# A transpose one place later in the job list, and a stage change without store waits, in an attention and FFN block

## The reference, cut to what matters

```python
xn = layernorm(x)                                  # x: 8 x 1024 x 512
# attention heads (head width 128)
local  = softmax(q_l k_l^T * s) v_l                # qkv = xn @ local_qkv_w
sparse = softmax(top102(q_s k_s^T * s)) v_s        # keeps the 102 largest scores of each row
xp     = xn @ memory_proj_w
w      = softmax(xp @ memory_bank^T)               # 64 memory slots: "memory weights"
mem    = concat(xp, w @ memory_bank) @ mem_out_w + mem_out_b
pred   = gelu((xn @ pred_in_w + b) @ pred1_w + b) @ pred2_w + b
s = concat(local, sparse, mem, pred) @ warboss_w + warboss_b
# FFN over the same xn, hidden width 2048
g = silu(relu(xn @ w1 + b1) @ w2 + b2)
out = x + s * g
```

## Time and profile before

| | |
|---|---|
| time, median of 3 runs | 2635.92 us (2635.5 to 2636.25) |
| the profiled execution's own time | 2635.15 us |
| its span, first to last instruction | 2633.3 us |
| TensorE busy | 2550.7 us, 97% |
| VectorE busy | 2308.2 us, 88% |
| ScalarE busy | 1367.4 us, 52% |
| GpSimd busy | 1102.4 us, 42% |
| mean granted TensorE clock | 0.993 |
| mean DMA rate | 214 GB/s |

### The profile page before, as it was taken

How to read it: one execution, slowest core, us unless ns; L and a number is a source line. 1 busy time by engine, 2 the same in 40 slices (tenths; PEclk the granted TensorE clock), 3 DMA queues, 4 the chain that set the end, 5 groups by cost and what they waited for, 6 DMA issues and landing times.

```text
span 2633.3 us, 37059 instructions
## 1 busy us (share of the span) xinstructions
PE 2550.7 (97%) x12900; PEld 2145.8 (81%) x12900; DVE 2308.2 (88%) x5217; ACT 1367.4 (52%) x2311; POOL 1102.4 (42%) x863
## 2 busy tenths in 40 slices
PE   6999999969999999999999999999999999999998
PEld 5887788757888888888888888888888888888886
DVE  7555555569999999999999999999999999999996
ACT  5777777734444444444444444444444444445443
POOL 4444444423344444444444444444444444444444
PEclk9999999989999999999999999999999999999999
DMA  6777777794556455655564556456655655465554
GB/s 214 289 288 291 291 271 272 275 355 148 192 183 238 167 194 192 226 173 195 202 230 166 192 196 229 160 199 212 211 179 183 235 189 197 164 241 175 195 168 165
DMA packets 168555, 562.29 MB, mean 214 GB/s; under 512 B 18161, under 2 KB 31665, under 8 KB 159921
## 3 DMA queue, kind: packets, MB, share of 16 engines
q1 hardware_dynamic: 168368, 559.91, 60.6%
HBM read 425.63 MB, written 134.22 MB: 213 GB/s over the span
## 4 chain that ended last, share of the span: by engine, by line
PE 76%; DVE 2%; DMA 1%; POOL 0%; issue 0%; ACT 0%; POOLq 0%; SPq 0%
PE acc L60 9%; PE acc L58 9%; PE hid L58 9%; PE hid L60 9%; PE acc L59 9%; PE hid L59 9%; PE o L60 5%; PE o L58 4%; PE o L59 4%; PE scores L1248 4%; PE scores L60 2%; PE scores L59 2%; PE scores L58 2%; DVE larger L1164 1%; DVE top_l L1144 1%; DMA w1s<-ffn_scratch 0%
## 5 line engine op out<-in xcount | busy, mean ns | idle before, releaser
L1004 POOL TENSOR_TENSOR h_lo<-h,h_hi 128x512 fp32r<-128x512 f32 x256 | 332.8, 1300 | 884.5 <-ACT h_hi L902 884.5
L1144 DVE MAX8 top_l<-larger 128x8 f32<-128x512 f32 x832 | 573.8, 690 | 13.2
L1164 DVE MATCH_REPLACE8 larger<-top_l,larger 128x512 f32<-128x512 f32 x768 | 519.3, 676 | 0.0
L901 ACT ACTIVATE h<-hid,b 128x512 f32<-128x512 f32 x256 | 176.7, 690 | 489.6 <-PE hid L60 489.6
L58 PE MATMUL acc<-w2s,h_hi 128*128 128x512 f32 x1024 | 412.1, 402 | 0.0
L58 PE MATMUL hid<-xnT,w1s 128*128 128x512 f32 x1024 | 400.4, 391 | 5.3 <-DMA w1s<-ffn_scratch 3.2
L60 PE MATMUL acc<-w2s,h_lo 128*128 128x512 f32 x1024 | 401.6, 392 | 0.0
L59 PE MATMUL acc<-w2s,h_hi 128*128 128x512 f32 x1024 | 400.2, 391 | 0.0
L60 PE MATMUL hid<-xnT,w1s 128*128 128x512 f32 x1024 | 400.1, 391 | 0.0
L59 PE MATMUL hid<-xnT,w1s 128*128 128x512 f32 x1024 | 399.2, 390 | 0.0
L1004 POOL TENSOR_TENSOR pT_s<-pT,pT_s 128x512 fp32r<-128x512 f32 x256 | 326.4, 1297 | 51.8 <-ACT pT_s L914 51.8
(11 more groups left out here) (170 smaller groups left out, 5575.4 us busy)
## 6 DMA issues: line engine op xcount, KB each, us to landing
w2s<-ffn_scratch SPq DMA_DIRECT2D x259, 512.0 KB, 3.9
w1s<-ffn_scratch SPq DMA_DIRECT2D x258, 512.0 KB, 4.5
kv<-kv_scratch SPq DMA_DIRECT2D x34, 1024.0 KB, 6.6
xnT<-xnT_scratch SPq DMA_DIRECT2D x68, 512.0 KB, 8.0
tl<-tile_scratch SPq DMA_DIRECT2D x66, 512.0 KB, 3.9
xnT_scratch<-xnT SPq DMA_DIRECT2D x16, 2048.0 KB, 13.6
kv_scratch<-kv_out SPq DMA_DIRECT2D x32, 1024.0 KB, 6.3
tile_scratch<-tiles_out SPq DMA_DIRECT2D x16, 2048.0 KB, 7.7
```

Of the source, the lines that this page charges most:

```text
L901: nc.scalar.activation(h32[:, c % 2, :], hid[:, :], ACT.Relu, bias=bias)
L1004: return nc.gpsimd.tensor_tensor(out_, value, hi_.bitcast(F32), ALU.subtract).then_inc(ready, 1)
L1144: l_step = count(nc.vector.max(top_l[:, own], larger[:, :]))
L1164: l_step = count(nc.vector.match_replace(larger[:, :], top_l[:, own], larger[:, :], LOWEST))
```

## The change

- `wt` stands behind `kl` in `JOBS`, not ahead of it. The other engines' written orders stay as they are.
- Stage 1 no longer waits for its stores to land. The semaphores of the K/V and tile stores live in both stages, and stage 2 waits on them ahead of the loads that read the last stores.
- In the last half (n = `LAST` = 15): no input load and no layer norm; behind the FFN store, and ahead of the tile store, SyncE loads stage 2's tile 0, K sparse of batch 0 and W1 chunk 0 into buffers that both stages share (`load_first`); there is no further FFN load; VectorE, not GpSimd, subtracts for `v23`.
- xnT is one buffer of both stages; half 0, which the last transposes leave there, isn't loaded again.
- Stage 2's first loads go in the order W1 chunk 1, (wait for the tile stores), W2 chunk 0, K local, W2 chunk 1, tile 1, (wait for the K/V stores). The other W2 chunk follows in the loop, and the loads of xnT move from tiles 0 and 4 of a batch to tiles 1 and 5.

```diff
-JOBS = ["mp", "pi", "ql", "ms", "p1a", "p1b", "qs", "wt", "kl", "ks", "p2",
+JOBS = ["mp", "pi", "ql", "ms", "p1a", "p1b", "qs", "kl", "wt", "ks", "p2",
...
+                def load_first():
+
+                    sp.wait_ge(kv_st, 32 * LAST)
+                    sp.wait_ge(tiles_st, 16 * LAST)
+                    loads = ((shared.tl0[:, :, :, :].rearrange("p i s n -> p (i s n)"),
+                              tile_d[0, :, :, :, :].rearrange("p i s n -> p (i s n)")),
+                             (shared.ks[:, :, :, :].rearrange("p u s n -> p (u s n)"),
+                              kv_d[0, :, U_KS:U_KS + 2, :, :].rearrange("p u s n -> p (u s n)")),
+                             (shared.w10[:, :, :].rearrange("p s n -> p (s n)"),
+                              ffn_d[0, :, W1, :, :].rearrange("p s n -> p (s n)")))
+                    for (to, of), ready in zip(loads, shared.first_in):
+                        sp.dma_start(to.bitcast(F32), of).then_inc(ready, 16)
...
-                        sp.wait_ge(xn_ready, n + 2)
-                        sp.dma_start(xin[:, :, :],
...
+                        if n < LAST:
+                            sp.wait_ge(xn_ready, n + 2)
+                            sp.dma_start(xin[:, :, :],
...
+                        if n == LAST:
+                            load_first()
...
-                        load_ffn((n + 1) & (CH - 1))
-
-                        sp.wait_ge(kv_l, 4 * n + 4)
+                        if n < LAST:
+                            load_ffn(n + 1)
+                            sp.wait_ge(kv_l, 4 * n + 4)
+                        else:
+                            sp.wait_ge(kv_l, 4 * n + 3)
+                            sp.wait_ge(last_v_l, 1)
                         store_kv(2)
...
                 sp.wait_ge(xnT_st, 16 * 2 * B)
-                sp.wait_ge(kv_st, 16 * 4 * B)
-                sp.wait_ge(tiles_st, 16 * 2 * B)
-                sp.wait_ge(ffn_st, 16 * 2 * B)
-                sp.wait_ge(ffn_in, 32 * (2 * B + 1))
...
-                        layer_norm(n + 2)
+                        if n < LAST:
+                            layer_norm(n + 2)
+                        else:
+                            c = slice(2 * P, 4 * P)
+                            dve.wait_ge(bank_read, done(n, "v23"))
+                            subtract(kv_out[:, 2:4, LOW, c], kv_out[:, 2:4, LOW, c].bitcast(F32),
+                                     kv_out[:, 2:4, HI, c]).then_inc(last_v_l, 1)
...
-                load_tl(0, 0, 0)
-                load_kv(U_KS, 0)
-                load_w1(0, 0)
-                load_xn(0, 0, 0)
                 load_w1(1, 1)
+                sp.wait_ge(tiles_st, 16 * 2 * B)
+                load_w2(0, 0)
                 load_kv(U_KL, 0)
-                for c in range(W2_RING - 1):
-                    load_w2(c, c)
+                load_w2(1, 1)
                 load_tl(1, 1, 1)
+                sp.wait_ge(kv_st, 16 * 4 * B)
```

## The result

The changed kernel takes 2714.2 us (2713.7 to 2714.7) against 2635.7 before: ratio 1.030, 95% interval 1.029 to 1.032. It is slower, as forecast, but by 78.5 us and not by 26.

The account below looks back on a forecast made before the run. The prediction took TensorE to bound the kernel, busy 2550.7 of 2633.3 us. Its terms were 2635.15 + 21.3 (longer halves) + 21 (clock) - 16.1 (stage change) = 2661.4, on the median 2662 us; whole range 2637 to 2668.

Parts of the forecast that it names:

- The moved wait: Stage 1: TensorE's wait for `wt` goes, one for gelu_lo before `p2` comes; each half 1.33 us longer, +21.3 us in all.
- The size of the wait, 2.7 us: Stage 1, before `p2`: `kl` copies and FFN split delay gelu_lo by 1.95 us, a stall of 2.84 us (2.7 shown).
- The clock, 1.4 us per half: Stage 1: TensorE's clock falls behind the new wait in nearly every one of 15 halves, +21 us, ends 0 and +27.
- The first rival: Stage 1: the stall comes as computed but TensorE's clock doesn't fall, 2641 us; chance 0.22.
- The stage change, -16.1 us: Between stages 1 and 2: early loads and dropped store waits gain 16.1 us, ends -13 and -18.5.
- e + 3.0: Stage change: first scores start 3.0 us after e, the end of the last V projection, 14.3 us sooner than before.
- the K store, expected at e - 9.5: Stage change: K store goes out about 9.5 us before the last V projection ends, so K lands near e + 2.
- the forecast's end of -13: Stage change: the smaller gain, if the block's end or a landing takes 3 us more.
- gelu_lo in time: Stage 1 rival: the delay stays within 0.62 us of slack, so the removed stall counts in full, 2599 us; chance 0.09.
- The stage change brings little: Stage change rival: late first operands or slow engines leave -5 in place of -16.1 us, 2673 us; chance 0.04.
- The range: Whole kernel: forecast's own range 2650 to 2671 us; whole range 2637 to 2668 us.
- the second one: Stage 1 rival that gelu_lo comes in time, 2599 us, chance 0.09; placed on the edge of no change, 2630.6 to 2641.2.

Follow-up runs that it names:

- e3: Changed kernel, but GpSimd begins its FFN subtraction only when VectorE has formed gelu_lo: 2667.1 us, ratio 1.013 to the kernel before.
- e9: Changed kernel with 20 filler matmuls ahead of TensorE's wait for gelu_lo, their product overwritten by `p2`: 2681.1 us, ratio 1.018 to the kernel before.
- e5: Changed kernel, but ScalarE's FFN split comes behind its copies of `wt`, not those of `kl`: 2650.1 us, ratio 1.007 to the kernel before.
- e1: Changed kernel with the old job order put back, so the stage change alone: 2619.9 us, ratio 0.995 to the kernel before.
- e4: Changed kernel, but VectorE forms gelu_lo ahead of its wait for `wt`, and act_hi after it: 2597.8 us, ratio 0.986 to the kernel before.
- e11: Kernel of before, but xnT is allocated ahead of the weights, as in the changed kernel: 2630.3 us, ratio 0.9985.
- e10: Kernel of before, but kv_out and tiles_out are allocated ahead of the stage's other buffers: 2633.0 us, ratio 1.000.

## Why the prediction was right in its direction and wrong in its size

- **The moved wait** ("Each half becomes longer"): right. The wait for `wt` is gone, the one for gelu_lo is there, and ScalarE's order shifted as worked out.
- **The size of the wait, 2.7 us**: wrong, 5.4. The failed step is "gelu_lo, which ends at 331.84, then ends at 333.79". It moved two VectorE instructions by 1.95 us and kept their durations, without asking what GpSimd does at the new time. The sentence "GpSimd gets `kl` and the FFN chunk sooner" stood there as a harmless by-product; it is what put a subtraction of 2.34 us and one of 1.28 (1.71 with its own wait) across them. That is 2.55 us per half, 41 us in all. `e3` shows the term as predicted once GpSimd is out of the way: 0.69, 1.23 and a wait of 2.84 us. The sign was already in the trace of before, unread, on GpSimd: the subtraction of K local takes 1.81 us beside gelu_lo, where the same one of K sparse takes 1.28.

```profile
331.18 1.81 POOL L314 TENSOR_TENSOR kv_out<-kv_out 128x512 fp32r<-128x512 f32 x1 [1.18 <-ACT kv_out L416]
332.95 2.39 POOL L314 TENSOR_TENSOR ffn<-ffn 128x1024 fp32r<-128x1024 f32 x1
335.30 1.28 POOL L314 TENSOR_TENSOR kv_out<-kv_out 128x512 fp32r<-128x512 f32 x1
```

- **The clock, 1.4 us per half**: the mechanism was right, also for the wait that the prediction took (`e3`: a wait of 2.84, 1.5 us of clock). With the longer wait it measured 2.3, or 2.2 by `e9`: some 15 us more in all. The first rival, that the clock stays, is refuted: in `e3` it fell in every half, and even with the 2.13 to 2.18 us of `e5` in 11 of 14. The rule of the Trainium skill that the prediction set against its row (TensorE: Matmul & The Clock Gate, HAM oscillation) would have kept the clock up at the 2.84 us of `e3`; the traces disagree with it.
- **The stage change, -16.1 us**: 17.5 measured, and that is luck. The first scores at e + 3.0 came at e + 2.95, and the 0.4 us for the block's end, which rested on no row, is about right (the last V store's issue ends at 631.13, stage 2's first load goes out at 631.60). But the K store, expected at e - 9.5 without a row for it, went out at e - 14.2, because stage 1 had lost more than forecast; the waits for W1 of up to 4 us never came. With halves as predicted (`e3`) it goes out at e - 8.5, and the gain is 70.4 - 58.0 = 12.4 us: the tile store alone lands at e + 10.2, where the prediction had the V store behind it through by e + 9.7; W1 chunk 1 then lands at e + 14.2, not at e + 11.0, and the local maximum starts at e + 27.0, not near e + 23. For that case the forecast's end of -13 was nearer than its -16.1. Without the new wait 11.2 (`e1`) and 9.5 us (`e4`) are left.
- **gelu_lo in time**: refuted, as worked out; the price of that case, 2599, is near what `e4` (2598) reaches by the edit that makes it true. Part of that is luck: the price counts 16.1 us for a stage change that gains 9.5 in `e4`, and 1.4 us per half (its own term is 1.51, which gives 2597) where the halves of `e4` are 1.8 us shorter than before.
- **The stage change brings little**: refuted; 9.5 us is the least that any run with it and without the store waits shows.
- **The rest**: halves are 0.25 us shorter by xnT's place, 4 us in all, which no step had.
- **The range**: its upper ends add up to 2635.9 + 23 + 27 - 13 = 2673, not 2671, and no sum is shown for the lower bound of 2650. The rival that sits on the edge at 2641 is the clock that stays, not the second one. Neither slip matters beside the 52 us missed.
- **The sum again**, with measured terms, per half: -1.5 for the wait removed, +5.55 for the new one, +2.3 of clock, -0.3 of place, 6.0; times 16 is 96, less 17.5, so 79 over before. In this sum the clock is what is left over; `e9` alone measures it, as 2.2. The range ended at 2668 because its upper bounds varied only terms that were on the list. The one between engines was not.

## What to carry to other kernels

When an instruction moves in time, its duration is not carried along: list what every other engine runs in the new slot, above all GpSimd beside a VectorE instruction with two operands in SBUF. In a job list that several engines share, a move changes the order only for those that walk the list; an engine whose order is written out keeps its old one, and its wait for the moved job then holds back whatever stands behind it, so move the independent result ahead of that wait. In this kernel a TensorE wait of 2.1 to 2.9 us in each round of the loop cost the wait and, on average, 1.2 to 1.5 us of low clock on top. And a gain at the end of a stage that was computed from another run's timing holds only for that timing: here it ranged from 9.5 to 17.5 us with how early the last stores went out.

## What the hardware showed unexpectedly

- A subtraction of VectorE and one of GpSimd, both from SBUF, exclude each other in either order: 0.69 became 2.29 us for VectorE, 2.34 became 3.45 us for GpSimd, and in `e5` a lead of 0.02 to 0.05 us decided that VectorE went first.
- The granted clock fell 0 to 1.4 us behind the end of a wait of 2.13 to 2.18 us between dense matmuls in 11 of 14 halves of `e5`, and stayed at 1.00 in the other three.
- Where xnT lies in SBUF changes the projection matmuls from 401 to 394 ns and a half of 31.45 us by 0.25 (`e11` against `e10`, on the assumption about the order of buffers above). Which property of the address does this is open; it wasn't tried.
